# Spectral vision tower on one core: signs of the mixing weights made on ScalarE, first modes requested by GpSimd, head's mixing visits behind the slot's first turn

## The chip, the cores and the metric

The kernel runs on one core of one Trainium2 chip. The metric is the device time of one execution in microseconds: 5875.86 us, the median of 3 runs (5870.03 to 5879.43).

## The reference, cut to what matters

128 images of 64 x 64 pixels with 3 channels are lifted to 32 channels and normed. Four layers follow; each adds a spectral convolution (12 x 12 low modes in two corners of the spectrum, each mode with its own complex 32 x 32 matrix) and a 1 x 1 convolution, and norms again. A head of three small matrix products makes one number per pixel, and an attention with an expert network ends the program.

```python
def spectral_conv(x, w1, w2):
    x_ft = jnp.fft.rfft2(x)
    out_ft = jnp.zeros((b, w1.shape[1], h, w // 2 + 1), dtype=x_ft.dtype)
    out_ft = out_ft.at[:, :, :M1, :M2].set(jnp.einsum('bixy,ioxy->boxy', x_ft[:, :, :M1, :M2], w1))
    out_ft = out_ft.at[:, :, -M1:, :M2].set(jnp.einsum('bixy,ioxy->boxy', x_ft[:, :, -M1:, :M2], w2))
    return jnp.fft.irfft2(out_ft, s=(h, w))
h = layer_norm(x @ fc0_w + fc0_b, ln0_g, ln0_b)
for i in range(LAYERS):                      # 4
    x1 = spectral_conv(h, w1r[i] + 1j * w1i[i], w2r[i] + 1j * w2i[i])
    x2 = jnp.einsum('bchw,oc->bohw', h, conv_w[i]) + conv_b[i][None, :, None, None]
    h = layer_norm(x1 + x2, ln_g[i], ln_b[i])
    if i < LAYERS - 1:
        h = gelu(h)
h = gelu(h @ fc1_w + fc1_b)
h = gelu(h @ fc2_w + fc2_b)
h = h @ fc3_w + fc3_b
# then: h + attention(layernorm(h)), h + experts(layernorm(h))
```

## The kernel before, in words

Four images make a quad, 32 quads a phase. Phase 0 is the stem, phases 1 to 3 the layers, phase 4 the head; the attention and the experts come after them and are not touched. The function `quads` writes the order for all engines: each engine has a `body(n, q, front, back1, back2, nxt, ph, ...)` for quad n = 32 ph + q. Its front part (lift or inverse transform and convolution) works on quad n, its back parts on quads n - 1 and n - 2 (turning, gelu, forward transform). A body has four slots k = 0 to 3. Engines meet only through semaphores and each works through its own queue in order.

In a slot of the stem or a layer TensorE does `turn_back` (L913), `turn_out` (L904), `lift` (L861) or `inv_h` and `conv` (L885, L892), twice for two halves wh; ScalarE `px` (L1126), `gelu` (L1133), `square` (L1117) and `keep_y` (L1121), twice; VectorE `normed` (L1254), `sums` (L1261), after odd slots the nine short steps of `rsqrt_half` (L1267 to L1283), and the turns `turn_z` (L1235), `turn_w` (L1241) and, in slot 2, `turn_modes` (L1247). GpSimd's `order_x` (L812) follows `turn_modes` and copies the modes into `x_out`, which SyncE stores to `xmodes`.

Weights. The mixing of a layer multiplies with `wslot` (mode, 4 sign slots, 32 output channels; neighbouring modes of one channel lie 128 floats apart). It is built during the phase before, in quads 8 to 23, one round per quad, by `expand` on GpSimd: eight DMAs of raw weights into `w1_raw` and `w2_raw` (L789), a wait for them, and then for each of two slots a memset of the last 12 modes (L796), `w1_raw` times a sign into `wslot` (L797), `w2_raw` times a sign in place (L799), and the reversed `w2_raw` added to `wslot` (L804). Rounds 0 to 7 make slots 0 and 3, rounds 8 to 15 slots 1 and 2. `expand` stands behind `order_x` in GpSimd's body.

Mixing. Four chunks of 8 quads have their modes mixed in four parts each (`PARTS`: 4, 3, 3 and 3 kx), one part per quad: chunks 0 and 1 in quads 24 to 31, chunks 2 and 3 in quads 0 to 7 of the next phase. A part has two visits, 2 kx in slot 1 and the rest in slot 3. A visit is `mix` on TensorE (L961, 12 products for one kx, 24 records) into `ps_f` and `mix` on VectorE (L1295, L1297), which centers the sums into `y_st`; SyncE stores these to `ymodes` (L718). The modes are loaded in two halves (kx below 7, and the rest) from `xmodes` by `load_part`, four DMAs on SyncE's queue (L710). For chunk 0 the first half is requested at the start of q = 24, the second at that body's end. Before the first visit of a chunk 0 TensorE waits for all weights (`w_step`) and for the half (`x_half`).

Head. There a slot is `head_slot`: fc1 (L976 into `ps_f`, L982 into `ps_s`), fc2 (L991), the turn of `xhat[1]`, the inverse transform, fc3 (L1000), convolution, fc2, the second fc1 and so on, with ScalarE's gelus g1 (L1140) and g2 (L1145) and VectorE's `take_xt` (L1303) and `take_tok` (L1314) between them. A mixing visit comes ahead of all of the slot; fc1 then waits for `mix_read`, since it writes the same `ps_f`.

Of the kernel before, what the change touches and what calls it, by code (L numbers as in the profile page):

```python
# [10 lines left out]
COMP = 4  # L11
# [15 lines left out]
def vit_tower(nc, x, p, cst, out, scratch):  # L27
# [5 lines left out]
    with ctx:  # L33
# [81 lines left out]
        def bank(name, shape=[128, 512]):  # L115
# [12 lines left out]
            "x_low", "x_high", "mix_done", "mix_sum", "mix_read", "w_raw", "w_step",  # L128
# [4 lines left out]
        x_half = [s["x_low"], s["x_high"]]  # L133
        primed = []
# [13 lines left out]

        block = ctx.enter_context(nc.Block())
# [3 lines left out]
        def quads(eng, body, unroll=False):  # L153

            def rest(ph, kind, nxt):
                if unroll:
                    for q in range(8, 24):
                        body(QUADS * ph + q, q, kind, kind, kind, kind, ph, mixed=KX * 4 * ph)  # L160
                else:
                    with eng.Fori(8, 24) as q:
                        body(QUADS * ph + q, q, kind, kind, kind, kind, ph, mixed=KX * 4 * ph)
# [469 lines left out]
        def _(sp):  # L633
# [70 lines left out]
            def load_part(half, seq, chunk, ph):  # L704
                then(sp, "mix_done", KX * (seq - 1) + (LOW_K if half == 0 else KX))
                then(sp, "xmodes_stored", 16 * (QUADS * ph + 8 * chunk + 8))
                m0, m1 = (0, LOW_K * M) if half == 0 else (LOW_K * M, MODES)
                src = xmodes[8 * chunk:8 * chunk + 8].rearrange("q (i c) (a m) -> a c (q i) m", i=4, a=COMP)
                for c in range(COMP):
                    sp.dma_start(xm[half][32 * c:32 * c + 32, :, :], src[c][:, :, m0:m1]).then_inc(x_half[half], 16)  # L710
# [19 lines left out]
            def body(n, q, front, back1, back2, nxt, ph, part=None, chunk=None, seq=None, mixed=0):  # L730
# [3 lines left out]
                if part == 0 and chunk == 0:  # L734
                    load_part(0, seq, chunk, source)
# [21 lines left out]
                if part is not None:  # L757
                    store_part(part, seq, chunk)
                    if part == 0:
                        load_part(1, seq, chunk, source)  # L760
# [13 lines left out]
        def _(pool):  # L774
# [8 lines left out]
            def expand(l, rnd):  # L783
                slots, parts = ((0, 3), "riir") if rnd < CH // OCH else ((1, 2), "irri")
                o0, done = rnd * OCH % CH, l * ROUNDS + rnd
                for c, part in enumerate(parts):
# [5 lines left out]
                wait(pool, "w_raw", 128 * done + 128)  # L792
                then(pool, "mix_done", KX * 4 * l)
                for i, sl in enumerate(slots):
                    dst = wslot[:, :, sl, o0:o0 + OCH].rearrange("p m o -> p o m")
                    nc.gpsimd.memset(dst[:, :, M * M:MODES], 0.0)  # L796
                    nc.gpsimd.tensor_scalar(dst[:, :, 0:M * M], w1_raw[:, :, :], c_sign[:, sl:sl + 1], None, ALU.mult  # L797
                                            ).then_inc(s["w_step"], 1)
                    nc.gpsimd.tensor_scalar(w2_raw[:, :, :], w2_raw[:, :, :], c_sign[:, 4 + sl:5 + sl], None,  # L799
                                            ALU.mult).then_inc(s["w_step"], 1)  # L800
                    then(pool, "w_step", 6 * done + 3 * i + 2)
                    view = dst[:, :, M:MODES].rearrange("p o (k m) -> p o k m", m=M)
                    rev = w2_raw[:, :, :].rearrange("p o (k m) -> p o k m", m=M)[:, :, ::-1, :]
                    nc.gpsimd.tensor_tensor(view, view, rev, ALU.add).then_inc(s["w_step"], 1)  # L804
                    then(pool, "w_step", 6 * done + 3 * i + 3)
# [9 lines left out]
            def body(n, q, front, back1, back2, nxt, ph, part=None, chunk=None, seq=None, mixed=0):  # L815
# [10 lines left out]
        def _(pe):  # L826
# [116 lines left out]
            def mix(part, chunk, seq, ph, k, count, tw_count, g1_count):  # L943

                k0 = PARTS[part][0]
                if k == 0 and part == 0 and chunk == 0:
                    pe.wait_ge(s["w_step"], 6 * ROUNDS * (ph + 1))
                    pe.wait_ge(s["bias_ready"], ph + 1)
                if k == 0 and part in (0, 2):
                    pe.wait_ge(x_half[part // 2], 64 * (seq + 1))  # L950
# [54 lines left out]
            def body(n, q, front, back1, back2, nxt, ph, part=None, chunk=None, seq=None, mixed=0):  # L1005
# [3 lines left out]
                for k in range(4):  # L1009
# [7 lines left out]
                    pair = 4 * (n - 1 - LAST) + k  # L1017
                    if part is not None and k % 2 == 1:
# [5 lines left out]
                        mix(part, chunk, seq, ph, k - 1, count, tw_count, 4 * pair - 1 if inner else 0)  # L1024
                    seen = mixed if part is None or k % 2 == 0 else mixed + (2 if k == 1 else PARTS[part][1] - 2)
                    turned = 2 * (4 * n + k - 3)
                    kind = front if k == 3 else back1
                    if inner:
                        head_slot(n, k, pair, turned, front, back2, kind, nxt, seen)
# [27 lines left out]
            def head_slot(n, k, pair, turned, front, back2, kind, nxt, seen):  # L1057
# [10 lines left out]
                fc1(v, 0, iw_count, seen)  # L1068
# [402 lines left out]
```

## Time and profile before

| | us |
|---|---|
| median of 3 runs | 5875.86 |
| profiled execution | 5870.29 |
| its span, first to last instruction | 5868.6 |
| TensorE busy | 5338.6 (91%) |
| VectorE busy | 4244.8 (72%) |
| ScalarE busy | 3689.6 (63%) |
| GpSimd busy | 1169.3 (20%) |
| granted TensorE clock, mean | 0.957 |

PE is TensorE's products, PEld its weight loads (an f32 product is two records), DVE VectorE, ACT ScalarE, POOL GpSimd, SPq SyncE's queue. Columns of a timeline: start in us from the span's start, us that the row lasts, engine, line, operation, output <- input, count of merged instructions, and in brackets how long the engine stood before and what ended it. Times are of one profiled execution. A busy share is an average over phases with different limits, so stretches are read one by one.

### The profile page before, as it was taken

The page shows a single profiled execution, that of the slowest core. Times are in us where ns is not written, and L with a number is a line of the kernel's source. Part 1 is how long each engine was busy: PE and PEld are TensorE (multiplying, and loading weights), DVE is VectorE, ACT ScalarE, POOL GpSimd, SP SyncE. Part 2 cuts the span into 40 slices and gives each one's busy share as a digit, 9 for nine tenths or more (in the row PEclk, how much of TensorE's full clock was granted, in tenths as well). Part 3 has the DMA queues.
Part 4 walks back from the last instruction along what each step waited for, and adds up shares of the span by engine and source line. Part 5 has one row for each costly group of instructions (what it writes and reads, how often), then busy time and mean ns, then how long its engine had stood idle before and what let it go on. Part 6 is the DMA issues. An engine that isn't in the chain of part 4 may idle for free.

```text
span 5868.6 us, 134909 instructions
## 1 busy us (share of the span) xinstructions
PE 5338.6 (91%) x43556; PEld 3021.4 (51%) x43556; DVE 4244.8 (72%) x7712; ACT 3689.6 (63%) x6005; POOL 1169.3 (20%) x1291
## 2 busy tenths in 40 slices
PE   5777789999999999999999999999999999878778
PEld 2444456666666666666666663333333333344343
DVE  5888789999898999899999884555555555444553
ACT  5777666667666677666677656567777777623333
POOL 0266300366200366200467100000000000000000
PEclk9998899999999999999999999999999999968898
DMA  1333467666777666777666772221111111000000
GB/s 66 115 124 120 139 170 225 206 213 210 215 215 218 202 213 214 215 211 226 211 212 211 215 196 66 62 63 51 51 51 51 51 52 51 20 1 7 7 7 4
DMA packets 427386, 756.21 MB, mean 129 GB/s; under 512 B 277809, under 2 KB 335922, under 8 KB 361530
## 3 DMA queue, kind: packets, MB, share of 16 engines
q1 hardware_dynamic: 410682, 714.26, 39.5%
q0 software_dynamic: 16384, 37.78, 2.2%
q8 instruction: 188, 3.08, 0.2%
q14 instruction: 132, 1.08, 0.1%
HBM read 397.49 MB, written 354.42 MB: 128 GB/s over the span
## 4 chain that ended last, share of the span: by engine, by line
PE 77%; DVE 10%; issue 6%; ACT 4%; SPq 1%; POOL 1%; DMA 1%; DVEq 0%; ACTq 0%; POOLq 0%
PE ps_y L892 17%; PE ps_t L904 9%; PE ps_y L885 9%; PE ps_t L991 8%; PE ps_t L913 7%; PE ps_f L926 4%; PE ps_f L976 4%; PE ps_s L939 2%; PE ps_f L961 2%; PE ps_s L871 2%; PE ps_t L1000 2%; PE ps_t L328 2%; PE ps_y L861 2%; DVE big L1254 1%; PE ps_f L318 1%
## 5 line engine op out<-in xcount | busy, mean ns | idle before, releaser
L1117 ACT ACTIVATE big<-ps_y 128x512 f32<-128x512 f32 x1280 | 773.9, 605 | 859.9 <-PE ps_y L892 784.8
L892 PEld LDWEIGHTS ps_y<-conv_now,big 128*128 128x128 f32 x8192 | 993.2, 191 | 520.2 <-issue 520.2
L1261 DVE TENSOR_REDUCE big<-big 128x16 f32<-128x512 f32 x1280 | 845.4, 678 | 531.6 <-ACT big L1117 531.3
L892 PE MATMUL ps_y<-conv_now,big 128*128 128x128 f32 x8192 | 1147.2, 283 | 0.0
L1254 DVE TENSOR_TENSOR big<-big 128x512 f32<-128x512 f32 x1280 | 878.4, 706 | 108.7 <-PE ps_t L904 102.5
L1126 ACT ACTIVATE big<-ps_t 128x512 f32<-128x512 f32 x1024 | 616.6, 602 | 474.0 <-PE ps_t L913 468.3
L904 PE MATMUL ps_t<-ident,big 128*128 128x128 f32 x5120 | 804.4, 281 | 88.5 <-DVE big L1254 86.5
L1133 ACT ACTIVATE big<-ps_t,g_now 128x512 f32<-128x512 f32 x1024 | 802.4, 784 | 63.1 <-PE ps_t L904 62.1
L1121 ACT ACTIVATE big<-ps_y 128x512 f32<-128x512 f32 x1280 | 776.1, 606 | 0.0
L904 PEld LDWEIGHTS ps_t<-ident,big 128*128 128x128 f32 x5120 | 596.3, 143 | 317.0 <-issue 207.2
L913 PE MATMUL ps_t<-ident,big 128*128 128x128 f32 x4096 | 662.0, 285 | 40.2 <-ACT big L1126 40.2
L913 PEld LDWEIGHTS ps_t<-ident,big 128*128 128x128 f32 x4096 | 457.9, 143 | 427.1 <-issue 293.7
L991 PE MATMUL ps_t<-big,fc_w 128*64 128x512 f32 x2048 | 558.6, 624 | 4.2 <-issue 3.3
L1241 DVE STREAM_TRANSPOSE big<-ps_f 128x1024 f32<-128x1024 f32 x256 | 508.1, 1985 | 23.3 <-issue 22.7
L812 POOL COPY x_out<-fw_sb 128x312 f32<-128x312 f32 x256 | 107.4, 448 | 2029.9 <-DVE fw_sb L1247 2029.9
L1145 ACT ACTIVATE big<-ps_t,fc_b 128x512 f32<-128x512 f32 x512 | 354.6, 693 | 122.9 <-PE ps_t L991 122.7
L926 PE MATMUL ps_f<-big,c_fwh 64*32 64x512 f32 x4096 | 364.1, 604 | 54.2 <-issue 40.4
L1303 DVE COPY w_raw<-ps_t 128x512 f32<-128x512 f32 x256 | 177.0, 692 | 271.2 <-PE ps_t L904 271.2
L1140 ACT ACTIVATE big<-ps_f,fc_b 128x1024 f32<-128x1024 f32 x256 | 286.8, 1120 | 107.1 <-PE ps_s L982 59.7
L797 POOL TENSOR_SCALAR wslot<-w_raw,c_sign 128x576 f32<-128x576 f32 x128 | 327.5, 2559 | 0.0
L976 PE MATMUL ps_f<-w_raw,fc_w 32*128 32x512 f32 x1024 | 292.0, 646 | 38.7 <-DVE y_st L1297 33.6
L982 PE MATMUL ps_s<-w_raw,fc_w 32*128 32x512 f32 x1024 | 292.6, 647 | 0.0
(179 smaller groups left out, 6775.9 us busy)
## 6 DMA issues: line engine op xcount, KB each, us to landing
hstore<-big SPq DMA_DIRECT2D x256, 1024.0 KB, 4.5
big<-hstore SPq DMA_DIRECT2D x256, 1024.0 KB, 5.1
xmodes<-x_out SPq DMA_DIRECT2D x128, 312.0 KB, 5.0
y_kt<-ymodes SPq DMA_DIRECT2D x512, 78.0 KB
ymodes<-y_st SPq DMA_DIRECT2D x192, 144.0 KB, 3.0
mix_room<-xmodes SPq DMA_DIRECT2D x64, 336.0 KB, 7.4
mix_room<-xmodes SPq DMA_DIRECT2D x64, 288.0 KB, 6.2
ymodes<-y_st SPq DMA_DIRECT2D x64, 192.0 KB, 3.3
```

Source lines behind the costliest of these rows:

```text
L885: mm(ps_y[64 * half:64 * half + 64, wh, :], c_inh[r, :], z_kx[j][r, 512 * odd:512 * odd + 512], start=True, stop=False)
L892: last = mm(ps_y[:, wh, 128 * b:128 * b + 128], h_in[k // 2][:, at:at + 128], conv_now[:, :], start=False, stop=(b == 3))
L904: last = nc.tensor.transpose(ps_t1[:, 128 * b:128 * b + 128], xhat[wh][:, 128 * b:128 * b + 128], ident[:, :])
L913: last = nc.tensor.transpose(ps_t2[:, 128 * b:128 * b + 128], h_new[k // 2][:, at:at + 128], ident[:, :])
L926: last = mm(ps_f[at:at + 32, odd, :], c_fwh[r, :], h_px[2 * odd + wh][r, :], start=True, stop=True)
L991: last = mm(ps_t2[64 * i:64 * i + 64, :], fc2_w[:, :], gelu1[2 * pr + i], start=True, stop=True)
L1117: af(y_sq[wh], ps_y[:, wh, :], ACT.Square).then_inc(s["sq_done"], 1)
L1121: af(y_sb[2 * k + wh], ps_y[:, wh, :], ACT.Copy).then_inc(s["y_read"], 1)
L1126: af(h_px[2 * (k % 2) + wh], ps_t2[:, :], ACT.Copy).then_inc(s["px_done"], 1)
L1133: af(h_new[k // 2][:, at:at + 512], ps_t1[:, :], ACT.Identity if kind == "stem" else ACT.Gelu, bias=g_now[:, 1:2], scale=g_now[:, 0:1]).th ...
L1254: v_.tensor_tensor(groups(xhat[wh]), groups(y_sb[2 * k + wh]), rstd[:, k // 2, at:at + 16].unsqueeze(2).to_broadcast([128, 16, 32]), ALU.m ...
L1261: v_.tensor_reduce(ss[:, k // 2, at:at + 16], groups(y_sq[wh]), AX.X, ALU.add).then_inc(s["ss_done"], 1)
```

## The change

The signs go to ScalarE. `expand` is split: GpSimd's `load_raw` requests the raw weights at the start of its body, ahead of `order_x`, and in round 0 clears the last 12 modes of all of `wslot` by one memset; behind `order_x` it does the two additions (`add_weights`). ScalarE's `sign_w1` and `sign_w2` make, as activations with a scale from `c_sign`, two signs into `wslot` and the first sign of `w2_raw` behind slot 1, and the second sign of `w2_raw` in slot 3 ahead of its first square. The loop over quads 8 to 23 becomes two loops, so that the pair of slots is fixed in each. The first chunk's modes are requested by GpSimd, one of eight DMAs in each of quads 16 to 23 (`load_first`); TensorE waits for them on semaphores of their own. SyncE's two requests of them fall away. In the head a visit stands behind the slot's first fc1, the second fc2 of the last pair and the turn of `xhat[1]`.

```diff
-            def expand(l, rnd):
-                ...
+            def load_raw(l, rnd, slots):
+                parts = "riir" if slots[0] == 0 else "irri"
+                o0, done = rnd * OCH % CH, l * ROUNDS + rnd
+                then(pool, "w_added", 2 * done)
+                ...
+                if rnd == 0:
+                    then(pool, "mix_done", KX * 4 * l)
+                    nc.gpsimd.memset(wslot[:, M * M:MODES, :, :], 0.0).then_inc(s["w_zero"], 1)
+            def add_weights(l, rnd, slot, second):
+                o0, done = rnd * OCH % CH, l * ROUNDS + rnd
+                then(pool, "w_scaled", 3 * done + 2 + second)
+                view, rev = weight_views(slot, slice(o0, o0 + OCH))
+                nc.gpsimd.tensor_tensor(view, view, rev, ALU.add).then_inc(s["w_added"], 1)
+            def load_first(ph, half, c):
+                mixed, stored = modes_wanted(half, 4 * ph, 0, ph)
+                then(pool, "mix_done", mixed)
+                then(pool, "xmodes_stored", stored)
+                pool.dma_start(*modes_part(half, 0, c)).then_inc(x_first[half], 16)
 # GpSimd's body
+                if slots is not None:
+                    load_raw(ph, q - 8, slots)
+                    if q >= 16:
+                        load_first(ph, (q - 16) // 4, q % 4)
                 if back2 in STORED:
                     order_x(n - 2)
-                if isinstance(q, int) and 8 <= q < 24 and front in STORED:
-                    expand(ph, q - 8)
+                if slots is not None:
+                    for second in range(2):
+                        add_weights(ph, q - 8, slots[second], second)
 # SyncE's body: load_part only for chunks 1 to 3
 # TensorE's mix
-                    pe.wait_ge(s["w_step"], 6 * ROUNDS * (ph + 1))
+                    pe.wait_ge(s["w_added"], 2 * ROUNDS * (ph + 1))
+                    if chunk == 0:
+                        pe.wait_ge(x_first[part // 2], 64 * (ph + 1))
 # TensorE's head_slot
-                fc1(v, 0, iw_count, seen)
+                fc1(v, 0, iw_count, mixed)
                 if not opening:
                     fc2(v - 1, 1)
                     turn_out(turned - 1, "head", 1, pair - 1)
+                if visit is not None:
+                    mix(*visit, 2 * v + 1)
 # ScalarE
+            def sign_w1(l, rnd, o, slots):
+                done = l * ROUNDS + rnd
+                wait(act, "w_raw", 128 * done + 128)
+                wait(act, "w_zero", l + 1)
+                for slot in slots:
+                    last = af(wslot[:, 0:M * M, slot, o].rearrange("p m o -> p o m"), w1_raw[:, :, :], ACT.Copy,
+                              scale=c_sign[:, slot:slot + 1])
+                last.then_inc(s["w_scaled"], 1)
+            def sign_w2(l, rnd, slot, second):
+                if second:
+                    wait(act, "w_added", 2 * (l * ROUNDS + rnd) + 1)
+                af(w2_raw[:, :, :], w2_raw[:, :, :], ACT.Copy, scale=c_sign[:, 4 + slot:5 + slot]).then_inc(s["w_scaled"], 1)
```

## Rows read from the trace of the kernel before

**Rows 1.** Busy us by stretch: stretch, length, each engine's busy us (count), PEclk, DMA share, GB/s.
```profile
106.92:243.65 136.73, 111.62 (x960) 63.11 (x960) 114.33 (x229) 111.17 (x205) 5.04 (x13) 0.95 0.30 115
243.65:633.99 390.34, 300.24 (x2404) 169.50 (x2404) 326.37 (x571) 281.09 (x515) 255.62 (x271) 0.90 0.36 123
1101.03:1486.81 385.78, 375.79 (x3243) 250.59 (x3242) 350.96 (x586) 269.84 (x480) 262.14 (x271) 1.00 0.63 211
3909.30:4250.14 340.84, 336.75 (x2076) 131.94 (x2072) 183.34 (x338) 244.28 (x337) 0.00 (x0) 1.00 0.18 56
```

**Rows 2.** The same table: intervals across q = 24 (stem, layer) and across q = 28.
```profile
633.99:671.31 37.32, 24.38 (x206) 14.91 (x206) 22.86 (x43) 17.03 (x33) 17.12 (x18) 0.73 0.52 124
1486.81:1523.50 36.69, 28.49 (x268) 19.28 (x267) 26.28 (x44) 18.02 (x33) 17.07 (x18) 0.91 0.73 186
1607.09:1635.27 28.18, 27.71 (x293) 19.01 (x292) 25.25 (x46) 17.97 (x32) 0.85 (x3) 1.00 0.60 195
```

**Rows 3.** Timeline of GpSimd, SyncE and TensorE at q = 24 of phase 1.
```profile
1507.63 1.78 POOL L804 TENSOR_TENSOR wslot<-wslot,w_raw 128x576 f32<-128x576 f32 x1
...
1491.05 7.08 SPq L710 DMA_DIRECT2D mix_room<-xmodes  x4
...
1509.75 0.62 PE L961 MATMUL ps_f<-wslot,mix_room 128*32 128x128 f32 x2 [7.72 <-POOL wslot L804]
```

**Rows 4.** Busy table again: the head's seven quads that have mixing visits.
```profile
3500.51:3909.30 408.79, 373.57 (x2614) 152.97 (x2618) 203.12 (x372) 248.30 (x336) 0.99 (x3) 0.96 0.25 59
```

**Rows 5.** Timeline in the head: a visit, and a slot without one.
```profile
3596.66 0.89 PE L961 MATMUL ps_f<-wslot,mix_room 128*32 128x128 f32 x24
...
3599.88 0.70 PE L976 MATMUL ps_f<-w_raw,fc_w 32*128 32x512 f32 x2 [2.32 <-DVE y_st L1297]
...
3943.96 1.13 ACT L1140 ACTIVATE big<-ps_f,fc_b 128x1024 f32<-128x1024 f32 x1
...
3949.08 0.70 PE L976 MATMUL ps_f<-w_raw,fc_w 32*128 32x512 f32 x2
```

**Rows 6.** Groups by line and shape: count, busy us, mean ns, idle before.
```profile
L797 POOL TENSOR_SCALAR wslot<-w_raw,c_sign 128x576 f32<-128x576 f32 x128 | 327.5, 2559 | 0.0
L804 POOL TENSOR_TENSOR wslot<-wslot,w_raw 128x576 f32<-128x576 f32 x128 | 255.4, 1995 | 14.8
L799 POOL TENSOR_SCALAR w_raw<-w_raw,c_sign 128x576 f32<-128x576 f32 x128 | 222.3, 1737 | 0.0
...
L789 POOL DMA_DIRECT2D w_raw<-in_tok_w1r x128 | 65.9, 515 | 8.9 <-issue 8.7
...
L1145 ACT ACTIVATE big<-ps_t,fc_b 128x512 f32<-128x512 f32 x512 | 354.6, 693 | 122.9 <-PE ps_t L991 122.7
```

**Rows 7.** Timeline of a layer's slot 2: ScalarE's first work and TensorE's turn.
```profile
1202.32 0.60 ACT L1126 ACTIVATE big<-ps_t 128x512 f32<-128x512 f32 x1 [1.52 <-PE ps_t L913]
...
1202.81 0.77 ACT L1133 ACTIVATE big<-ps_t,g_now 128x512 f32<-128x512 f32 x1
...
1204.91 0.47 PEld L904 LDWEIGHTS ps_t<-ident,big 128*128 128x128 f32 x4
```

**Rows 8.** Timeline: stem quad without weights, VectorE beside an addition, beside a sign.
```profile
175.18 0.84 POOL L812 COPY x_out<-fw_sb 128x312 f32<-128x312 f32 x2 [22.68 <-DVE fw_sb L1247]
...
176.75 1.27 DVE L1254 TENSOR_TENSOR big<-big 128x512 f32<-128x512 f32 x2
...
177.48 0.66 PE L904 MATMUL ps_t<-ident,big 128*128 128x128 f32 x4 [1.35 <-DVE big L1254]
...
474.39 1.84 POOL L804 TENSOR_TENSOR wslot<-wslot,w_raw 128x576 f32<-128x576 f32 x1
474.41 1.91 DVE L1277 SCALAR_TENSOR_TENSOR big<-big 128x64 f32<-128x64 f32 x1
...
1214.06 2.26 POOL L797 TENSOR_SCALAR wslot<-w_raw,c_sign 128x576 f32<-128x576 f32 x1
...
1215.11 0.22 DVE L1271 TENSOR_TENSOR big<-big 128x64 f32<-128x64 f32 x1
```

More of the change, by code:

```diff
@@ L147, in then, with modes_wanted, modes_part, weight_views @@
                 eng.nop(nofuse=True)
+        def modes_wanted(half, seq, chunk, ph):
+            return KX * (seq - 1) + (LOW_K if half == 0 else KX), 16 * (QUADS * ph + 8 * chunk + 8)
+        def modes_part(half, chunk, c):
+            m0, m1 = (0, LOW_K * M) if half == 0 else (LOW_K * M, MODES)
+            src = xmodes[8 * chunk:8 * chunk + 8].rearrange("q (i c) (a m) -> a c (q i) m", i=4, a=COMP)
+            return xm[half][32 * c:32 * c + 32, :, :], src[c][:, :, m0:m1]
+        def weight_views(slot, cols):
+            dst = wslot[:, M:MODES, slot, cols].rearrange("p (k m) o -> p o k m", m=M)
+            return dst, w2_raw[:, :, :].rearrange("p o (k m) -> p o k m", m=M)[:, :, ::-1, :]
         block = ctx.enter_context(nc.Block())
@@ L157, in rest @@
             def rest(ph, kind, nxt):
[L158 to L163, printed above, removed]
+                for base, slots in ((8, (0, 3)), (16, (1, 2))):
+                    if unroll:
+                        for q in range(base, base + 8):
+                            body(QUADS * ph + q, q, kind, kind, kind, kind, ph, mixed=KX * 4 * ph, slots=slots)
+                    else:
+                        with eng.Fori(base, base + 8) as q:
+                            body(QUADS * ph + q, q, kind, kind, kind, kind, ph, mixed=KX * 4 * ph, slots=slots)
                 for q in range(24, 32):
@@ L758, in body @@
                     store_part(part, seq, chunk)
-                    if part == 0:
+                    if part == 0 and chunk != 0:
                         load_part(1, seq, chunk, source)
@@ L791, in expand @@
                                        ).then_inc(s["w_raw"], 16)
[L792 to L805, printed above, removed]
+                if rnd == 0:
[11 more added lines that the diff above has]
+                pool.dma_start(*modes_part(half, 0, c)).then_inc(x_first[half], 16)
             def order_x(m):
@@ L1023, in body @@
                             tw_count = 2 * n - 1 if back1 in STORED else 2 * LAST
-                        mix(part, chunk, seq, ph, k - 1, count, tw_count, 4 * pair - 1 if inner else 0)
-                    seen = mixed if part is None or k % 2 == 0 else mixed + (2 if k == 1 else PARTS[part][1] - 2)
+                        visit = (part, chunk, seq, ph, k - 1, count, tw_count)
+                    if visit is not None and not inner:
+                        mix(*visit, 0)
                     turned = 2 * (4 * n + k - 3)
@@ L1084, in head_slot @@
                 fc2(v, 0)
-                fc1(v + 1, 1, iw_later, seen)
+                fc1(v + 1, 1, iw_later, mixed if visit is None else mixed + visit[5])
                 if kind is not None:
@@ L1192, in body @@
                             gelu(turned + wh, m, kt, wh, kind)
+                        if slots is not None and k == 3 and wh == 0 and front in STORED:
+                            sign_w2(ph, q - 8, slots[1], 1)
                         if front is not None:
@@ L1195, in body @@
                             keep_y(unit + wh, k, wh)
+                    if slots is not None and k == 1 and front in STORED:
+                        sign_w1(ph, q - 8, bass.ds(4 * q - 8 * 4 if slots[0] == 0 else 4 * q - 16 * 4, OCH), slots)
+                        sign_w2(ph, q - 8, slots[0], 0)
             take_x(0)
@@ L1322, in body @@
                     inner = back1 == "head"
-                    if part is not None and k % 2 == 1:
-                        mix(part, seq, k - 1, 2 if k == 1 else PARTS[part][1] - 2)
+                    visit = (part, seq, k - 1, 2 if k == 1 else PARTS[part][1] - 2) if part is not None and k % 2 == 1 else None
+                    if visit is not None and not inner:
+                        mix(*visit)
                     if inner:
-                        head_slot(n, k, unit, turned, front, back2, kind, nxt, fresh, m, kn)
+                        head_slot(n, k, unit, turned, front, back2, kind, nxt, fresh, m, kn, visit)
                         continue
@@ L1362, in head_slot @@
                         normed(late + 1, 2 * n - 2 + (k + 1) // 2, (k + 1) % 4, 1)
+                if visit is not None:
+                    mix(*visit)
                 if k == 0 and front in MIXED:
```

35 lines of the change are left out of this document (17 added, 18 removed).

## The prediction

> **What bounds the kernel now.** I read the busy table by stretches first. The ends of its stretches are starts of marks that come at a fixed place in each quad: GpSimd's copy into `x_out` (once, in slot 2) in the stem and the layers, VectorE's turn of the inverse transform (twice, slots 0 and 2) in the head. See three things in [rows 1]. The layers' rounds (15 quads in 385.78 us, 25.72 each) and the head without mixing (7 quads in 340.84, 48.69 each) have TensorE busy for 97 and 99%: there only TensorE's own work and its stalls count, and ScalarE has some 115 us of air in 385.78. The stem is different: six quads without weights take 22.79 each, the 15 with weights 26.02, TensorE is busy for 77%, and its granted clock falls from 0.95 to 0.90. Then I took the intervals that stick out, and the timeline inside them.
>
> First, the quad where each phase's mixing begins (q = 24). The interval between marks across it is 37.32 in the stem and 36.69 in the first of the three layers, against 28.18 at q = 28, which mixes as well [rows 2]. Inside it TensorE stands 7.72 us until GpSimd's last addition to `wslot` [rows 3]: this addition starts only at 1507.63, since the last round's raw weights are requested after slot 2 of q = 23 and have to land before two times memset, sign, sign and addition. SyncE's four requests for the first modes start at 1491.05 and last 7.08 us, so these would be next in line.
>
> Second, the head's seven quads with mixing: 408.79 us [rows 4] against the 340.84 without, 67.95 more. The mixing of one kx is 24 TensorE records in 0.89 us; but the next fc1 starts 3.2 us after the mixing's first record and has stood 2.32 for VectorE's y_st [rows 5]. TensorE has nothing queued between them, since fc1 writes the same `ps_f`.
>
> **The change part by part.**
>
> *The stall at q = 24.* Now the signs of round 23 are made in slots 1 and 3 of q = 23, the last addition (2.00 us [rows 6]) ends early in q = 24, before slot 1's mixing, and the first half of the modes was requested in q = 16 to 19, the second in q = 20 to 23. Both halves of the edit are needed: with only the signs moved, modes requested from 1491 to 1498 would still be late. What is left is the interval of q = 28 less one kx of mixing, 28.18 - 0.83 = 27.35 (0.83 chosen a little under the 0.89 of [rows 5], whose last record overlaps what follows). In a layer that gives back 36.69 - 27.35 = 9.34, three times (I take the other two like the first); in the stem the reference is a round of 26.02 plus a 2-kx visit of 1.8, so 9.5. Sum 37.5 us. Bounds: 30 (only the 7.72 each) to 42. Next in line in q = 24 is plain TensorE work.
>
> *The head's visits.* Fourteen visits, 22 kx, move behind fc1(v, 0), fc2 and the turn of xhat[1]. They now need `ps_f` free from ScalarE's gelu of this very fc1: in an unmixed slot that gelu takes 1.13 us from 3943.96, and fc2 and the turn in TensorE's queue cover most of it, so I add 0.3 per visit. The fc1 that needs `ps_f` again starts at 3949.08 in the unmixed slot [rows 5], after inv_h, fc3, conv and fc2, some 4 us later, against 2.3 us that VectorE takes for two kx. So the round trip is hidden and only 22 x 0.89 = 19.6 plus 14 x 0.3 = 4.2 stay: 67.95 - 23.8 = 44.2 us gained. Bounds: 55 (two thirds of 0.89 per kx, as the records overlap with their neighbours, and no waits) and 20 (if VectorE, with its take_xt and normed ahead of the visit and take_tok behind it, keeps 1.7 us of each). SyncE stores the modes some 3 us later in the slot; the next thing behind them on its queue waits for the slot's end anyway.
>
> *Signs on ScalarE.* Each of the 64 rounds adds four activations of 576 columns. The nearest row is fc2's gelu, 693 ns for 512 columns with one pointer operand [rows 6]; scaled by columns that is 0.78. Two of the four write `wslot` with 512 bytes between neighbours. No ScalarE row shows such a write. GpSimd's sign takes 2559 ns into `wslot` and 1737 into `w2_raw` [rows 6]. I bound the strided activation by 0.78 and 2.56 and take 1.0: GpSimd's factor is 1.47, which would make 1.15 of 0.78, and its row holds the stretches that VectorE gives it. The burst behind slot 1 is then 0.78 + 2 x 1.0 = 2.8 us. In the layers ScalarE stands 1.52 us there, and its next gelu ends at 1203.58 where TensorE's turn that needs it is at 1204.91 [rows 7]: 1.33 more, so 2.85 are free. The fourth activation fits before slot 3's square. Cost in the layers: 0.
>
> The Trainium skill speaks against this part ("SBUF — State Buffer", Door 1: each access that goes to a new 16-byte line pays a penalty). No run here shows it for ScalarE; by the rates that the skill's "Vector Engine (DVE) Microarchitecture Reference" gives in its section on the access granule, an estimate would be 1.2 to 1.6 us per strided activation.
>
> *GpSimd's lighter load.* It loses memset and two signs per slot and keeps two additions. Its additions hold VectorE: a 64-column step that should take 0.23 us took 1.91 beside an addition of 1.84 [rows 8], while another ran its 0.22 us in the middle of a sign [rows 8]. The first addition now always starts when order_x is done. Put into the clean stem quad [rows 8]: order_x 175.18 to 176.02, addition to 177.9, so the normed that starts at 176.75 ends at about 178.4 instead of 177.4, and TensorE, which already stood 1.35 us for it, stands 1.0 longer. ScalarE's burst shifts slot 2 by 1.1 to 1.5 but runs into the same stall, so I don't add it; the second addition and the fourth activation I put at 0.5. A stem round is then 22.8 + 1.5 = 24.3, and with 0.5 for the traffic of the raw weights 24.8, against 26.02: 16 x 1.25 = 20 us gained. Bounds: 45 (all of 26.02 - 22.79, less little) and -10 (both additions hit, burst not covered). In the layers TensorE is idle for 10 of 385.78 us in 15 quads, so no more than 32 over 48 could come back, and the held normed is needed about when it comes: I take 3 us gained, between 15 gained and 20 lost.
>
> The Trainium skill ("SBUF — State Buffer", Who interferes with whom) has it that a VectorE instruction with two SBUF inputs and a GpSimd one that reads SBUF exclude each other for a whole instruction. The addition's row agrees; the sign's doesn't, since that step ran at its own speed inside it. By the rule alone the four signs that go would have held VectorE too, and the gain here would be nearer to the 45.
>
> *Eight pieces of modes on GpSimd.* Its requests of raw weights take 0.515 us for 32 rows each [rows 6]. A piece has 32 x 32 = 1024 runs. Below: 0.5 us. Above, if all of 0.5 were per run: 16 us. GpSimd now has air from the last raw request (about 4 us behind the second addition) to order_x in the next slot 2, about 13 us. I take 6, hidden; 16 would delay order_x by 3. The skill ("DMA: Bandwidth & Descriptors", Anatomy of one DMA) says that many descriptors can be emitted before a further cost shows; no row here shows it. The split of the loop 8 to 23 into two costs nothing that the trace shows at a loop's start.
>
> **Sum.** 37.5 + 44 + 20 + 3 = 104.5. The profiled execution took 5870.29 (span 5868.6); the median of the runs is 5875.86, 5.6 above. 5870.3 - 104.5 = 5766, and with a part of that distance 5768.
>
> **The rivals.**
>
> 1. *The signs bind ScalarE; slower.* If the strided activation costs what GpSimd's does, 2.56, the burst is 5.9 us. ScalarE's queue holds px, gelu and square behind it, and TensorE and VectorE wait for these. Beyond 2.85 us each of 48 layer rounds loses 3.05 (146 us), each of 16 stem rounds some 3.5 (56): 5768 + 202 = 5970. It decides from where it eats the 104.5: a burst of about 4.5, 1.85 per strided activation. For: GpSimd's factor of 1.5, the skill's rule. Against: 1.85 is 2.4 times the contiguous price. 6%.
> 2. *The additions keep the stem where it is.* They land on the chain rsqrt, turn, normed each time instead of now and then: no gain in stem and 15 lost in layers, 5768 + 38 = 5806. For: [rows 8]. 20%.
> 3. *The head's wait moves.* fc1's second turn waits for y_st, 1.7 a visit: 5768 + 24 = 5792. For: VectorE has three more pieces between. Against: the 4 us. 12%.
> 4. *Descriptors bind GpSimd.* At 16 us a piece the second addition is late for the next raw weights: 32 quads by 1 to 3, say 60: 5828; it would be slower than before only from 20 us a piece. 9%, a third of it at or beyond no change.
>
> **How the numbers follow.** The forecast has 53%. Its own spread is the stem's and the head's, 5745 to 5790; with rivals 2 to 4 the range is 5730 to 5830, which leaves rival 1, the tail of 4 and a full gain in all parts outside. A measurement of this kernel tells 0.2% (12 us) from no change. Faster: 53 + 20 + 12 + 5 = 90%; within: 3%; slower: 7%.
>
> **What would show it.** The interval across q = 24 at 27 to 28 us and no TensorE wait for `wslot`; visits in the head followed directly by inv_h, and seven quads in 360 to 368 us; four activations per round of 0.8 to 1.1 us with ScalarE's wait ahead of slot 2's px gone; VectorE's normed of slot 2 at 1.6 us in every round; stem rounds near 24.8. Wrong if a strided activation is over 1.8 us, if a GpSimd request of modes is over 13 us, if layer rounds grow beyond 26, or if ScalarE waits for `w_raw`.

## The result, and the profile after

The changed kernel takes 5731.24 us (median of 4 runs, 5729.36 to 5733.41) against 5873.60 beside it (4 runs, 5870.03 to 5879.43): ratio 0.9763, 95% interval 0.9751 to 0.9775. The profiled execution took 5729.41 us with a span of 5727.7, 140.9 under that of before, where 104.5 had been worked out. TensorE is busy for 5285.1 us (92%), VectorE 4230.7, ScalarE 3896.4 (68%), GpSimd 630.8 (11%).

First the busy table of the changed kernel by stretches, with the columns of [rows 1]. Its rows are, in order: the clean part of the stem, the stem's 15 rounds with weights, the interval across q = 24 of the stem, the 15 rounds of the first layer, its interval across q = 24, and the head's seven quads with mixing. They answer to [rows 1], [rows 2] and [rows 4]; the head without mixing (48.69 a quad) is as it was.

```profile
105.73:242.25 136.52, 110.76 (x954) 62.48 (x955) 114.36 (x229) 112.21 (x205) 10.43 (x22) 0.95 0.32 120
242.25:601.30 359.05, 286.29 (x2402) 159.17 (x2401) 300.80 (x571) 325.44 (x571) 132.86 (x188) 0.94 0.41 141
601.30:627.32 26.02, 21.91 (x218) 13.08 (x216) 22.30 (x43) 20.78 (x40) 4.50 (x5) 0.93 0.27 102
1051.19:1431.74 380.55, 373.03 (x3242) 250.72 (x3241) 354.65 (x586) 319.04 (x541) 134.34 (x188) 1.00 0.68 221
1431.74:1459.13 27.39, 26.88 (x269) 18.36 (x268) 25.84 (x44) 19.07 (x35) 4.57 (x5) 1.00 0.52 179
3403.97:3766.61 362.64, 358.10 (x2614) 148.04 (x2618) 203.32 (x371) 245.75 (x336) 0.98 (x3) 1.00 0.27 66
```

See two things in each row: the length less TensorE's busy time (how long it stood), and the busy time itself for the same count of records (how fast it was clocked). In the stem's rounds TensorE stood 90.1 us before and 72.8 now, and its 2404 records went from 300.2 busy at a granted clock of 0.90 to 286.3 at 0.94. In the head it stood 35.2 and now 4.5, and the same 2614 records went from 373.6 at 0.96 to 358.1 at 1.00. Both halves count.

What ended TensorE's waits in the stem's 15 rounds, before and after (us in total, times, longest): normed by VectorE, and ScalarE's px.

```profile
PE ps_t L904 <- DVE big L1254: 59.8, 29, 4.4
PE ps_t L913 <- ACT big L1126: 22.1, 31, 0.7
...
PE ps_t L926 <- DVE big L1302: 25.7, 30, 1.4
PE ps_t L935 <- ACT big L1155: 39.5, 44, 1.3
```

The wait for normed fell by 34 us, the wait for ScalarE, which now has the burst of signs ahead of px, grew by 17.

By marks at each quad's first square I split the 140.9: the stem's 16 rounds gave 33, the rest of the stem 6, the four quads where mixing begins 11.1, 9.4, 9.2 and 10.1 (40), the 48 rounds of the layers 5.1, 4.6 and 6.6 (16), the head's seven quads with visits 46. The attention and the experts, which the change does not touch, took 1.7 more.

At q = 24 of the layer (GpSimd, and TensorE's first mixing) neither weights nor modes are waited for; the last addition has been done for 7.6 us.

```profile
1432.55 1.86 POOL L816 TENSOR_TENSOR wslot<-wslot,w_raw 128x576 f32<-128x576 f32 x1
...
1437.48 1.90 POOL L816 TENSOR_TENSOR wslot<-wslot,w_raw 128x576 f32<-128x576 f32 x1 [3.07 <-ACT w_raw L1188]
...
1446.98 0.43 PE L986 MATMUL ps_f<-wslot,mix_room 128*32 128x128 f32 x2
```

Then a head slot with a visit. fc1 is followed by fc2, the turn, the visit and inv_h; the fc1 that needs `ps_f` again comes 3.26 us after VectorE's last step on it began.

```profile
3441.91 0.70 PE L1001 MATMUL ps_f<-w_raw,fc_w 32*128 32x512 f32 x2
...
3444.80 0.89 PE L986 MATMUL ps_f<-wslot,mix_room 128*32 128x128 f32 x24 [0.15 <-issue]
...
3445.63 1.09 PE L907 MATMUL ps_y<-z_second,c_inh 32*64 32x512 f32 x8
...
3446.48 0.56 DVE L1345 SCALAR_TENSOR_TENSOR y_st<-big,ps_f 128x384 f32<-128x384 f32 x1
...
3449.74 0.70 PE L1001 MATMUL ps_f<-w_raw,fc_w 32*128 32x512 f32 x2
```

Next ScalarE's burst in a layer. The rows overlap a little, so its length is read from starts: two strided signs from 1199.56 to 1201.71, the contiguous one to 1202.35, 2.79 us in all. ScalarE no longer stands before px, and its gelu ends 0.26 ahead of the turn (L926) that needs it.

```profile
1199.56 2.40 ACT L1181 ACTIVATE wslot<-w_raw,c_sign 128x576 f32 x2
...
1201.71 0.80 ACT L1188 ACTIVATE w_raw<-w_raw,c_sign 128x576 f32<-128x576 f32 x1
1202.35 0.65 ACT L1155 ACTIVATE big<-ps_t 128x512 f32<-128x512 f32 x1
1202.83 0.84 ACT L1162 ACTIVATE big<-ps_t,g_now 128x512 f32<-128x512 f32 x1
...
1203.93 0.60 PE L926 MATMUL ps_t<-ident,big 128*128 128x128 f32 x4
```

The groups of the changed kernel (count | busy us, mean ns | idle before):

```profile
L1181 ACT ACTIVATE wslot<-w_raw,c_sign 128x576 f32 x128 | 153.8, 1326 | 0.0
L1188 ACT ACTIVATE w_raw<-w_raw,c_sign 128x576 f32<-128x576 f32 x128 | 99.1, 775 | 0.0
L822 POOL DMA_DIRECT2D mix_room<-xmodes x32 | 25.8, 805 | 2.6 <-issue 0.9
```

### The profile page after: what moved, and what is told of

The parts are those of the page before. It is cut to its first block, busy times and chain, and to the rows that moved or that the text cites. A ratio compares the mean times of both kernels' runs of the same rounds, so it can differ in the third digit from the quotient of the medians.

```text
span 5727.7 us, 135011 instructions
## 1 busy us (share of the span) xinstructions
PE 5285.1 (92%) x43556; PEld 2997.1 (52%) x43556; DVE 4230.7 (74%) x7712; ACT 3896.4 (68%) x6261; POOL 630.8 (11%) x943
## 4 chain that ended last, share of the span: by engine, by line
PE 81%; DVE 9%; issue 5%; ACT 3%; SPq 1%; DVEq 0%; ACTq 0%; DMA 0%
PE ps_y L914 18%; PE ps_y L907 9%; PE ps_t L926 9%; PE ps_t L1016 8%; PE ps_t L935 8%; PE ps_f L948 4%; PE ps_f L1001 3%; PE ps_s L893 3%; PE ps_f L986 3%; PE ps_s L961 3%; PE ps_t L1025 2%; PE ps_t L346 2%; PE ps_y L883 2%; ACT big L1169 1%; PE ps_f L336 1%
## 5 line engine op out<-in xcount | busy, mean ns | idle before, releaser
L1302 DVE TENSOR_TENSOR big<-big 128x512 f32<-128x512 f32 x1280 | 932.1, 748 | 69.3 <-PE ps_t L926 62.2
L926 PE MATMUL ps_t<-ident,big 128*128 128x128 f32 x5120 | 790.5, 277 | 43.9 <-DVE big L1302 42.5
L926 PEld LDWEIGHTS ps_t<-ident,big 128*128 128x128 f32 x5120 | 587.6, 142 | 260.9 <-issue 204.8
L935 PE MATMUL ps_t<-ident,big 128*128 128x128 f32 x4096 | 654.4, 283 | 55.9 <-ACT big L1155 55.9
L935 PEld LDWEIGHTS ps_t<-ident,big 128*128 128x128 f32 x4096 | 453.6, 142 | 435.5 <-issue 312.5
L1169 ACT ACTIVATE big<-ps_s,fc_b 128x1024 f32<-128x1024 f32 x256 | 288.3, 1126 | 0.0
```

The costliest lines, as they stand in the source:

```text
L926: last = nc.tensor.transpose(ps_t1[:, 128 * b:128 * b + 128], xhat[wh][:, 128 * b:128 * b + 128], ident[:, :])
L935: last = nc.tensor.transpose(ps_t2[:, 128 * b:128 * b + 128], h_new[k // 2][:, at:at + 128], ident[:, :])
L1169: af(h_new[0][:, 1024 * half:1024 * half + 1024], src, ACT.Gelu, bias=fc1_b[:, :]).then_inc(s["g1_done"], 1)
L1302: v_.tensor_tensor(groups(xhat[wh]), groups(y_sb[2 * k + wh]), rstd[:, k // 2, at:at + 16].unsqueeze(2).to_broadcast([128, 16, 32]), ALU.m ...
```

## Experiments

Two questions were open: why the stem gave 33 and not 20, and where 16 us in the layers came from. Theory A: what sets the stem's rounds is VectorE's step held by the first addition (normed of slot 2). Rival B: ScalarE's burst. Theory C: before, GpSimd's signs stretched VectorE's rsqrt steps. Rival D: its additions did. Where a part of the weights' work is left out, the text says so.

### One part undone: the head's visits in front again

```diff
-                    if visit is not None and not inner:
+                    if visit is not None:
                         mix(*visit)
...
```

> The changed kernel with the head's mixing visits ahead of the slot again. The seven head quads with visits go back from 362 to 408 us, all else stays: 5731 + 46 = 5777. Rival (part of the head's gain came from the signs or from SyncE's lighter queue): less than 40 comes back.

5764.63 us (5761.11 to 5767.79), ratio to before 0.9819 (0.9804 to 0.9834). The head's seven quads with visits grew by 42.8 us. The medians differ by 33 only (the profiled executions by 38); the untouched attention part took 784.8 us here and 796.7 in the changed kernel. The head's seven quads, and that last part:

```profile
3411.62:3817.09 405.47, 370.31 (x2614) 152.39 (x2618) 203.13 (x372) 248.07 (x336) 0.98 (x3) 0.97 0.25 59
4981.26:5766.10 784.84, 604.00 (x3360) 305.37 (x3356) 372.19 (x819) 271.88 (x330) 0.00 (x0) 0.83 0.03 6
```

So the new order is worth 43 in the head: 30.6 less standing (35.2 here, 4.5 there) and 12.2 of busy time at the higher clock. The other 3 of the 46 are busy time too (373.6 before, 370.3 here, at 0.96 and 0.97). The last part moves by up to 12 us from kernel to kernel (784.8 to 797.3 over all profiles); why was not tested, and totals are read with that in mind.

### One part undone: the first modes requested by SyncE

```diff
+                if part == 0 and chunk == 0:
+                    load_part(0, seq, chunk, source)
...
-                    if q >= 16:
-                        load_first(ph, (q - 16) // 4, q % 4)
...
```

> The changed kernel with the first chunk's modes requested by SyncE again, at q = 24, as in the kernel before; signs and head as changed. Theory (both halves of the edit are needed): requested from about the start of q = 24 and 7 us long, they land some 4 us after TensorE's first visit wants them: q = 24 takes 32 to 33 us instead of 28.8 in each of four phases, 14 to 18 us in all, time 5745 to 5750. Rival (the loads were hidden, only the weights were late): q = 24 stays, time 5731 to 5733.

5746.57 us (5743.79 to 5747.46), ratio 0.9790 (0.9775 to 0.9805): 15 slower than the change. The quads where mixing begins took 4.0, 1.7, 1.6 and 5.1 us more, 12.4 in all. Q = 24 of the layer (SyncE and TensorE):

```profile
1446.07 5.81 SPq L727 DMA_DIRECT2D mix_room<-xmodes  x4
...
1458.53 0.41 PE L983 MATMUL ps_f<-wslot,mix_room 128*32 128x128 f32 x2 [1.48 <-DMA mix_room<-xmodes]
```

With the weights in time the modes are next in line, as the prediction had it. The wait is smaller than expected: most of the 40 us at q = 24 belongs to weights that are ready in time (signs moved, raw weights requested earlier), and 12 to the pieces on GpSimd.

### One piece moved: the first addition ahead of the copy of modes

```diff
+                if slots is not None:
+                    add_weights(ph, q - 8, slots[0], 0)
                 if back2 in STORED:
                     order_x(n - 2)
```

> The changed kernel with GpSimd's first addition of a round ahead of order_x instead of behind it. Theory A (the first addition holds VectorE's normed of slot 2, and in the stem TensorE waits for that normed): the addition then lies beside VectorE's turns, which it does not hold; that normed takes 1.3 us for two again, the stem's rounds fall from 23.9 to about 23.1, the layers' stay at 25.35, the time falls by 8 to 15 us to about 5720. Rival B (the stem's rounds are set by ScalarE's burst of signs behind slot 1, for which TensorE waits 1.25 us): the normed is free and the rounds stay at 23.9, time within 4 us of 5731.

5722.71 us (5719.04 to 5727.15), ratio 0.9751 (0.9738 to 0.9764). To tell it from the change, both were run again, on one chip.

> The changed kernel itself, run beside the kernel with the first addition ahead of the copy of the next rows, on one chip, to tell whether their times differ. Theory A (the held normed of slot 2 costs the stem's rounds about 0.4 us each): 5731 us, 6 to 9 us over the other. Rival (the two differ only by what the clock and the attention part do from one kernel to the next): both within 3 us of each other, near 5727.

> The changed kernel with the first addition of each round ahead of the stem's copy of rows (only the order differs, nothing is left out), a second time and beside the changed kernel. Theory A: 5723 us, with the rounds of the stem some 6 us shorter in sum than the changed kernel's and the layers the same. Rival: both within 3 us of each other.

5732.15 us for the change (5728.91 to 5735.42; 0.9769, 0.9756 to 0.9783) and 5722.16 for this kernel (5712.63 to 5730.74; 0.9750, 0.9733 to 0.9767). The intervals overlap, but the medians are 8.5 and 10.0 us apart, and the stem's 16 rounds say the same: 381.5 and 385.6 against 374.9 and 375.6. It is the fastest kernel of this study. The stem, first the change, then this kernel:

```profile
410.29 1.86 POOL L816 TENSOR_TENSOR wslot<-wslot,w_raw 128x576 f32<-128x576 f32 x1
...
411.09 2.21 DVE L1302 TENSOR_TENSOR big<-big 128x512 f32<-128x512 f32 x2
...
412.75 0.66 PE L926 MATMUL ps_t<-ident,big 128*128 128x128 f32 x4 [0.74 <-DVE big L1302]
```

```profile
407.87 1.85 POOL L816 TENSOR_TENSOR wslot<-wslot,w_raw 128x576 f32<-128x576 f32 x1 [10.55 <-ACT w_raw L1189]
...
408.39 1.95 DVE L1290 STREAM_TRANSPOSE big<-ps_f 128x1024 f32<-128x1024 f32 x1
...
410.16 1.47 DVE L1303 TENSOR_TENSOR big<-big 128x512 f32<-128x512 f32 x2
```

An addition that lies inside VectorE's turn out of PSUM costs that turn nothing (1.95 us, as anywhere), where inside the two normed it costs 0.9 (2.21 against the 1.27 of [rows 8]); the copy of modes, which now meets them, costs 0.2. In whole time theory A came true (8 to 15 us expected), but the stem's rounds fell from 23.9 to 23.5 and 23.6, half of the way to the 23.1 expected: TensorE stands 64.3 us in 15 rounds instead of 72.8 and 71.7.

### The additions left out

```diff
-                nc.gpsimd.tensor_tensor(view, view, rev, ALU.add).then_inc(s["w_added"], 1)
+                pool.sem_inc(s["w_added"], 1)
```

> The changed kernel with the two additions of each round left out (the weights lack their second corner). It shows what the additions cost. Theory A: no VectorE step is held; the stem's rounds fall from 23.94 to about 23.0, the layers' stay at 25.35, since what was held there had room. If the additions cost time in the layers too, their rounds fall below 25.3.

5724.56 us (one execution); the stem's 16 rounds 378.4, the layers' first 16 rounds 405.6 (406.0 with additions). The stem's 15 rounds:

```profile
244.34:598.37 354.03, 291.24 (x2402) 161.01 (x2401) 286.34 (x571) 324.04 (x571) 77.62 (x159) 0.92 0.41 143
```

TensorE stands 62.8 us in them, hardly less than with the addition in its better place, and a round takes 23.6, not the 23.0 expected. What keeps it from the 22.8 of the quads without weights [rows 1] is not standing (4.2 us a quad in both) but TensorE's busy time: 19.4 us a quad for the same 160 records, at 0.92, against 18.6 at 0.95. So the full burst of signs is in this kernel and costs no standing in sum, which speaks against B. In the layers, where the additions hold normed of slots 2 and 3 (VectorE is busy for 354.7 us in 15 rounds with them and 332.3 without, 1.5 a round), taking that away gives nothing: the rounds are 25.35 us either way.

### The same on the kernel before

```diff
-                    nc.gpsimd.tensor_tensor(view, view, rev, ALU.add).then_inc(s["w_step"], 1)
+                    pool.sem_inc(s["w_step"], 1)
```

> The kernel before with GpSimd's additions left out; signs and memsets stay. Theory C: the stretched steps stay, so the layers' rounds stay at 25.6 or more and the stem's above 25. Rival D: the layers' rounds fall to about 25.4 and the stem's to about 24.

The weights are signed by GpSimd as before, and not added. 5800.74 us (one execution), 66 under the kernel before beside it (5866.94). The stem's 16 rounds fell from 414.5 to 375.8 and the layers' from 411.1, 410.6 and 408.6 to 405.9, 405.9 and 402.4: in the layers the values of the changed kernel, in the stem 6 us less, with all signs still on GpSimd. The first layer's 15 rounds:

```profile
1058.38:1438.90 380.52, 373.08 (x3243) 250.79 (x3242) 340.24 (x586) 268.57 (x480) 193.19 (x241) 1.00 0.63 214
```

The signs still hold VectorE here, by 8 us in 15 rounds (340.2 against the 332.3 with neither), and the rounds are as short as without. So C falls as a cause by itself and D stands.

### The signs left out of the kernel before

```diff
-                    nc.gpsimd.tensor_scalar(dst[:, :, 0:M * M], w1_raw[:, :, :], c_sign[:, sl:sl + 1], None, ALU.mult
-                                            ).then_inc(s["w_step"], 1)
-                    ...
+                    nc.gpsimd.memset(dst[:, :, M * M:MODES], 0.0).then_inc(s["w_step"], 2)
```

> The kernel before with GpSimd's signs left out (raw weights are added to zeros); the two additions and memsets stay on GpSimd. Question: what did the layers' 0.35 us per round and the stem's 2.1 us come from. Theory C (the signs stretch VectorE's 64-column steps, which stand on the chain to the next normed): the rounds fall to about 25.4 and 24.5. Rival D (the additions did it, where they fell on the steps of rsqrt): with the additions left they stay above 25.6 and 25.5 unless they now fall elsewhere, which the trace shows. q = 24 loses some 6 us of its stall per phase in both.

5938.30 us (one execution), slower than before, with less work. (This kernel also clears the weights once at the start.) The layers' 16 rounds took 451.0, 440.9 and 444.5; the stem's are 25.4 each, where C had 24.5; q = 24 lost 3 to 4 us, not 6. Its rounds of the layer in the busy table, and the timeline in one (GpSimd, VectorE, TensorE):

```profile
1083.73:1508.89 425.16, 391.15 (x3239) 260.70 (x3238) 374.26 (x586) 270.19 (x480) 132.62 (x211) 0.96 0.57 191
```

```profile
1204.50 1.84 POOL L802 TENSOR_TENSOR wslot<-wslot,w_raw 128x576 f32<-128x576 f32 x1
...
1205.09 1.30 DVE L1265 TENSOR_SCALAR big<-big 128x64 f32<-128x64 f32 x1
...
1206.79 1.87 POOL L802 TENSOR_TENSOR wslot<-wslot,w_raw 128x576 f32<-128x576 f32 x1
...
1206.99 1.75 DVE L1271 TENSOR_TENSOR big<-big 128x64 f32<-128x64 f32 x1
...
1212.81 0.66 PE L902 MATMUL ps_t<-ident,big 128*128 128x128 f32 x4 [1.54 <-DVE big L1252]
```

TensorE stands 34 us in 15 rounds (10 before, [rows 1]), 26.3 of them for normed, and its clock falls to 0.96. Without the signs between them the two additions come at once, and in 14 of the 15 rounds they fall on two of the nine rsqrt steps, which end in what all of slot 2 waits for. Where an addition falls, not how much GpSimd does, sets its price.

### One addition early, one sign later

```diff
-                then(pool, "w_scaled", 3 * done + 2 + second)
+                then(pool, "w_scaled", 4 * done + 2 + 2 * second)
...
-                for slot in slots:
+                for slot in slots[0:1]:
...
+                        if slots is not None and k == 2 and wh == 0 and front in STORED:
+                            sign_w1b(...)   # the other slot's sign of w1
```

> As e3, and the second sign into wslot moves from behind slot 1 to slot 2, between ScalarE's first gelu and square, so that the burst behind slot 1 is 2.0 instead of 3.2 us. If the burst bounds the stem's rounds (rival B), they fall to 23.0 to 23.4 and the time to about 5715; if only the held normed does (theory A), nothing changes against e3. In the layers ScalarE waits over 1 us before the square of slot 2 in the kernel before, so 25.35 stays in both.

5781.43 us (5768.51 to 5789.44), ratio 0.9848 (0.9833 to 0.9863), a loss of 50 against the change. The shorter burst lets the early addition start too soon, and in the first layer it meets the last but one rsqrt step in 14 of 15 rounds and the last in one. A layer round is 25.85 instead of 25.35, the stem's 16 rounds 409.6.

```profile
1106.98 1.83 POOL L816 TENSOR_TENSOR wslot<-wslot,w_raw 128x576 f32<-128x576 f32 x1 [11.32 <-ACT w_raw L1193]
1107.12 1.77 DVE L1336 SCALAR_TENSOR_TENSOR big<-big 128x64 f32<-128x64 f32 x1
...
1112.57 0.66 PE L927 MATMUL ps_t<-ident,big 128*128 128x128 f32 x4 [0.26 <-DVE big L1309]
```

Two things changed here, the addition's place and the place of a sign on ScalarE. The layer's waits point to the first: TensorE now stands for normed in all 15 rounds (4.1 us in sum, none in the kernel with the early addition alone), and no wait for ScalarE was added.

### The burst made shorter

Contiguous signs (they go to the wrong places of the weights), one execution and then several; and signs over a quarter of the columns, for which every sign takes `[:, 0:1, :]` of its operands.

```diff
-                    last = af(wslot[:, 0:M * M, slot, o].rearrange("p m o -> p o m"), w1_raw[:, :, :], ACT.Copy,
+                    at = 0 if slot == slots[0] else OCH * M * M
+                    last = af(wflat[:, at:at + OCH * M * M].rearrange("p (o m) -> p o m", o=OCH), w1_raw[:, :, :], ACT.Copy,
```

> The changed kernel with ScalarE's two signs of w1 per round written to neighbouring floats instead of 512 bytes apart (so the first corner's weights are not what is computed). The strided store is the difference between 1.33 us and a contiguous 0.78: the burst behind slot 1 falls from 3.2 to 2.2 us. Rival B expects the stem's rounds to fall by up to 1 us (23.94 to 23.0), theory A by under 0.2, since TensorE's next stall for normed takes it up.

> The changed kernel with the two signs of w1 written to neighbouring columns, once more and in several runs; the signs go to the wrong places, so the weights are not the right ones. If the single look was one bad execution: stem's rounds 382 to 386 us and 5731 us, as the changed kernel. If the contiguous writes themselves shift the stem: again 390 to 397 us and 5740 to 5745 in each run.

> The changed kernel with ScalarE's four signs over one of the four output channels (144 of 576 columns), so the burst behind slot 1 should fall from 3.4 to about 1.2 us; it leaves out the sign of three quarters of the weights. Additions, loads and order unchanged (and the weights are cleared once at the start, as with the contiguous signs). Theory A (the stem's rounds are set by VectorE's held steps and by the clock, not by the burst): the stem's 16 rounds stay at 378 to 388 us, layers 406, whole time 5722 to 5735. Rival B (the burst sets the stem's rounds): 16 rounds near 365 us, whole time under 5716. If the kernel with contiguous signs was slow in the stem because a shorter burst moves the additions onto worse steps of VectorE or lowers the clock, this one is slow too: stem's rounds 390 or more.

Contiguous: 5742.13 (one execution), then 5743.29 us (5739.62 to 5745.08), ratio 0.9783 (0.9767 to 0.9799). A quarter: 5741.02 us (5730.06 to 5747.39), 0.9775 (0.9756 to 0.9794). These intervals overlap that of the change (0.9756 to 0.9783), so the argument rests on the stem in the profiles. Layers 405.6 to 405.8, as with the full burst. The stem's 16 rounds took 393.7 and 398.2, and 395.9: longer than the 381.5 and 385.6 with the full burst. B, which expected them shorter, falls. The stem's 15 rounds of the quarter signs, and what ended TensorE's waits in them:

```profile
243.46:615.39 371.93, 294.07 (x2400) 166.94 (x2400) 300.58 (x571) 294.55 (x571) 134.69 (x189) 0.91 0.40 136
```

```profile
PE ps_t L928 <- DVE big L1304: 49.6, 30, 2.3
PE ps_t L937 <- ACT big L1157: 21.4, 30, 0.7
```

The shorter burst does what it should, the wait for ScalarE falls from 39.5 us to 21.4; but the wait for normed, next in line, grows from 25.7 to 49.6. The additions did not move to worse steps: VectorE's busy time is the change's (300.6 against 300.8), and each round has one normed held by 0.9 us, as there. TensorE's busy time is 7.8 higher for as many records, at 0.91 where the change has 0.94, and it stands 77.9 against 72.8. Both kernels also clear the weights once at the start, and what leads to the lower clock stays open.

## Why the prediction was right

The time lay inside the range, 37 us below the forecast. Nothing cancelled: the stem and the layers gave 13 more each than forecast, the head and q = 24 some 2 each, and 6 came in the rest of the stem, which the sum left out. By its own steps:

*The stall at q = 24.* 37.5 forecast, 40 measured. The intervals, 37.32 and 36.69 before [rows 2], are 26.02 in the stem (under the 27 to 28 named) and 27.39 in the layer. Both halves of the edit were needed, as argued, though modes on SyncE would have cost only 12 of the 40.

*The head's visits.* 44.2 forecast, 46 measured (43 by the kernel that undoes the order). The order of events is the one foretold, and rival 3 did not come: no fc1 waits for `y_st`. What stays of the mixing was put at 23.8 us in seven quads, 3.4 each; they take 51.8 against the unmixed 48.7, 3.1 more. What the prediction did not say is that a third of the gain (15.5 of 46.2) is TensorE's busy time at the higher clock; using the unmixed quads, at 1.00, as the reference had put it into the sum unnoticed, which was luck.

*Signs on ScalarE.* The burst was put at 2.8 us and is 2.79; strided signs start 1.08 apart (1.0 taken). The row's mean is 1326 ns against 775 contiguous, inside the bounds though above the 0.8 to 1.1 us named as a sign. The layers' rounds are the same with a quarter of the columns, so nothing in them waits for it, and rival 1 fell.

*The pieces of modes.* 805 ns each, under the 6 us taken and near the lower bound. Rival 4 fell. (Of its 9% a third was no gain, so the chance of faster should have counted 6 and not 5; this changes nothing.)

*The stem.* 20 forecast, 33 measured (24.8 a round forecast, 23.9 found). The failing term is "A stem round is then 22.8 + 1.5 = 24.3, and with 0.5 for the traffic". It counted steps held and left out what the granted clock would do. Of the 31.3 us that 15 rounds gave, 14.0 are TensorE's busy time, at 0.94 instead of 0.90, and 17.3 less standing (28.8 and 10.4 in the second profile of the change). The held normed is real: moved away, it gives the other kernel some 8 us more. Nor did the additions before land on the chain "now and then": counted in the trace, one of them met an rsqrt step in 11 of the stem's 15 rounds, by 1.5 to 1.7 us each ([rows 8] has one), and none does in the changed kernel. The kernels without additions, before and changed, both have 23.6 a round, so all of the gap from there to 26.0 hung on them.

*The layers.* 3 forecast, 16 measured, over the part's own bound of 15. The failing step is "and the held normed is needed about when it comes". It is not needed then: with VectorE held by 1.5 us a round, the layers run at 25.35, as without any addition. What the additions cost before, 0.35 a round (25.72 [rows 1]; gone without them), came from other places in the round, though they held VectorE by less in sum (351.0 us busy [rows 1] against 340.2 without them, 11 in 15 rounds; 22 after). Part of it can be placed: TensorE stood for normed in 5 of the 15 rounds, 2.1 us in sum, and in none after. The longest round (26.89) has an addition on the first rsqrt step, whose own time is 0.20:

```profile
PE ps_t L904 <- DVE big L1254: 2.1, 5, 0.9
...
1122.88 1.84 POOL L804 TENSOR_TENSOR wslot<-wslot,w_raw 128x576 f32<-128x576 f32 x1
1123.04 1.74 DVE L1267 TENSOR_SCALAR big<-big 128x64 f32<-128x64 f32 x1
```

In other long rounds (up to 25.95) a sign held the first or second rsqrt step by 0.3 to 0.4 us; what sign and addition share there was not pinned down. The bound by TensorE's idle time was too tight as well: of the 5.2 us that these 15 rounds gave, 2.5 are less standing and 2.8 less busy time at a clock of 1.00 in both, for as many records, which overlap more. Rival 2 had the additions landing "on the chain rsqrt, turn, normed each time"; they do land on a normed each time, and in the layers that place is free. The dear place, rsqrt, is what the kernel without signs and the one with the early addition ran into.

The Trainium skill ("SBUF — State Buffer", Who interferes with whom) gives one rule for all GpSimd work that reads SBUF, beside a VectorE instruction with two SBUF inputs. For the additions the rows of such steps agree: 1.77 us beside 1.83, 1.75 beside 1.87. But an addition also held a step with one input (1.74 beside 1.84, the row above), so two inputs are not what it takes in this case. For the signs the rule does not hold for the whole instruction: a step ran its 0.22 us inside one [rows 8], and counted over that trace, rsqrt steps that started in the first 0.5 us of a sign were mostly held, by 0.3 to 0.5 us, while nearly all that started over 0.6 us behind its start ran at their own speed. That the turn out of PSUM is spared (1.95 beside an addition of 1.85) agrees with a rule about SBUF inputs.

## What to carry to other kernels

Where GpSimd's two-input work holds VectorE, do not count its microseconds; find on which VectorE step it starts in each round, since the same 1.85 us cost a round nothing on a step with slack, 0.5 us on a late step of a short dependent chain and some 3 us for two such hits, and removing work ahead of it can move it from the one to the other. When a stall of TensorE goes, count its busy time at the clock of an undisturbed stretch too: here that was 14 of 31 us (10 of 29 in a second profile) and 15 of 46. And when one wait of two in line is shortened, look at the other: signs over a quarter of the columns took 18 us off the wait for ScalarE and put 24 on the wait for VectorE.

## What was not expected of the hardware

In the stem the same records cost TensorE 286 us at a granted clock of 0.94 and 299 at 0.90 (contiguous signs, 15 rounds), with the same VectorE work. A mean of 0.94 over 359 us is, as an estimate from the row, some 43 us at the lower of the clock's two levels (1.2 and 2.4 GHz), and 0.90 over 374 us some 75. All three profiles with a shortened burst have the lower clock (0.90 or 0.91, against 0.93 and 0.94 in the two of the change), but lighter ScalarE work does not explain it by itself: the kernel with the early addition and the later sign has the full work and 0.90, and the kernel before without additions has less work and 0.92. A cause is not shown. The attention part, the same instructions in all kernels, took from 784.8 to 797.3 us.
